# The seam between feed-forward 0 and attention 1: parts of q and k handed over piece by piece, and the first maxima multiplied one block earlier

## The reference

```
x = x + ffn0(layernorm(x))        # gate, up and down projections; every operand is rounded to
                                  # 4-bit floats in blocks of 16 first; hidden width 352
x = x + attention1(layernorm(x))
    q, k, v = x Wq, x Wk, x Wv    # 16 heads of 8 features
    a = q k^T / sqrt(8), causal mask, softmax over keys
    out = (a v) Wout
```

## Time and profile before

| what | value |
|---|---|
| time, median of 3 runs | 934.86 us (933.84 to 935.25) |
| profiled execution: time, span | 932.55 us, 930.8 us |
| PE busy | 842.5 us (91%) |
| DVE busy | 728.3 us (78%) |
| ACT busy | 528.7 us (57%) |
| POOL busy | 465.4 us (50%) |
| mean granted clock of TensorE | 0.98 |

### The profile page before, as it was taken

How to read it: one execution, slowest core, us unless ns; L and a number is a source line. 1 busy time by engine, 2 the same in 40 slices (tenths; PEclk the granted TensorE clock), 3 DMA queues, 4 the chain that set the end, 5 groups by cost and what they waited for, 6 DMA issues and landing times. The chain is left out here.

```text
span 930.8 us, 17280 instructions
## 1 busy us (share of the span) xinstructions
PE 842.5 (91%) x5977; PEld 556.6 (60%) x5977; DVE 728.3 (78%) x1455; ACT 528.7 (57%) x771; POOL 465.4 (50%) x620
## 2 busy tenths in 40 slices
PE   5899999999778886689999999888889999999997
PEld 4677777775566655334444444443558767776875
DVE  6888998879899995888898998987666656565542
ACT  4677788789566675367777777767423223222311
POOL 4133222224568786236666666456464365345444
PEclk9999999999999999779999999999989999999999
DMA  9300000000000006765545446200000000000000
GB/s 284 93 12 12 11 11 11 0 13 0 16 1 12 1 12 130 142 129 117 111 82 126 106 85 127 52 4 14 12 1 24 1 23 23 23 0 23 11 12 12
DMA packets 36067, 43.79 MB, mean 47 GB/s; under 512 B 4878, under 2 KB 28094, under 8 KB 36000
## 3 DMA queue, kind: packets, MB, share of 16 engines
q1 hardware_dynamic: 36000, 42.93, 19.5%
HBM read 21.81 MB, written 15.09 MB: 40 GB/s over the span
## 5 line engine op out<-in xcount | busy, mean ns | idle before, releaser
L1877 ACT ACTIVATE PT<-PS 128x1024 f32<-128x1024 f32 x160 | 161.5, 1022 | 61.6 <-PE PS L1668 61.3
L1939 POOL TENSOR_SCALAR_AFFINE_SELECT PT<-PT 128x256 f32<-128x256 f32 (+1 forms) x224 | 97.3, 451 | 101.9 <-ACT PT L1877 99.9
L2368 POOL TENSOR_TENSOR PRE_sb<-PRE_sb,VA 128x512 f32<-128x512 f32 x64 | 82.3, 1285 | 125.8 <-DVE PRE_sb L2436 125.7
L2335 ACT ACTIVATE sg_d<-PS 128x512 f32<-128x512 f32 x64 | 38.1, 597 | 154.5 <-PE PS L1397 154.5
L2436 DVE TENSOR_TENSOR PRE_sb<-sg_d,PS 128x512 f32<-128x512 f32 x64 | 44.0, 688 | 79.6 <-ACT sg_d L2335 79.1
L465 ACT ACTIVATE E<-PS,m 128x512 f32<-128x512 f32 x128 | 85.7, 688 | 34.7 <-PE PS L351 25.8
L1979 DVE TENSOR_REDUCE negm<-PS 128x2 f32<-128x1024 f32 x64 | 77.8, 1221 | 20.0 <-PE PS L1657 19.6
L1684 PE MATMUL PS<-PT,VA 128*32 128x512 f32 (+3 forms) x1024 | 89.9, 446 | 3.6 <-POOL PT L1939 3.6
L1650 PE MATMUL PS<-kS,qS 52*128 52x384 bf16 (+3 forms) x512 | 64.3, 311 | 14.7 <-ACT PT L1877 6.9
L514 POOL TENSOR_SCALAR Qs<-Qs 128x1024 f32<-128x1024 f32 x32 | 34.5, 1080 | 81.6 <-ACT Qs L446 81.0
L1668 PE MATMUL PS<-qS,kS 55*128 55x384 bf16 (+3 forms) x512 | 63.4, 307 | 7.5 <-DVE negm L1979 3.5
(11 more groups left out here) (331 smaller groups left out, 2249.5 us busy)
## 6 DMA issues: line engine op xcount, KB each, us to landing
qk_rows<-parts SPq DMA_DIRECT2D x32, 192.0 KB, 2.8
qS<-qk_rows SPq DMA_DIRECT2D x32, 192.0 KB, 4.3
kS<-qk_rows SPq DMA_DIRECT2D x32, 192.0 KB, 4.6
xs_sb<-XN_sb SPq DMA_DIRECT2D x20, 256.0 KB, 2.3
qk_rows<-parts SPq DMA_DIRECT2D x32, 128.0 KB, 2.8
X_sb<-in_x_dram SPq DMA_DIRECT2D x8, 256.0 KB, 6.6
qk_rows<-parts SPq DMA_DIRECT2D x32, 64.0 KB, 2.5
out_dram<-X_sb SPq DMA_DIRECT2D x8, 256.0 KB, 2.3
```

Of the source, the lines that this page charges most:

```text
L1877: nc.scalar.activation(PT[:, quad % 2, u, :], PS[:, b:b + 2, :].rearrange("p b n -> p (b n)"), ACT.Exp).then_inc(exp_ready, 1)
L1939: nc.gpsimd.affine_select(out=v, in_=v, pattern=[[0, 4 if u == 4 else 2], [1, P]], compare_op=ALU.is_ge, fill=0.0, base=0, channel_multipl ...
L2368: nc.gpsimd.tensor_tensor(acts[:, s, f, :], acts[:, s, f, :], W[:, slot, s, :], ALU.mult).then_inc(weighted, 1)
```

## The change

Five things are changed, all in the seam.

1. The third parts of sequence 0 (`third_part(pool, 0, m)`) move on POOL from behind `rescale_h(LAST - 1, 1)` to before it.
2. A new function `both_parts_to_rows` takes the place of two calls of `parts_to_rows`, for sequences 0, 1 and 2. It issues the same 12 transfers, but in the order in which parts come to exist: behind the first part of q, the first part of k, the second of q, and so on.
3. The first four units of maxima of sequence 0 move into `last_turn` of feed-forward 0 on PE, behind `down(i, 0)`, behind the projection of k, behind `turn_h(i, 1)` and behind `down(i, 1)`. They alternate between the bank pairs 3, 4 and 1, 2. Their reductions stand at the end of DVE's list of that block.
4. In the opening the remaining 16 units are numbered from 4, and the work between them stands behind other units: v of sequence 0 behind 4, the turn of x behind 5, the projections behind 7 and 9, the turn of the maxima behind 11, v of sequence 1 behind 13 instead of 8. The ring of bank pairs runs the other way round.
5. On ACT `keep_v(0, 0)` stands behind the second parts of sequence 1 instead of before them, and `keep_maxima(0, 0)` before `keep_v(1, 1)` and two constants instead of behind them.

```diff
+    def both_parts_to_rows(self, sp, n, slot):
+
+        for k, part in ((1, self.part1), (2, self.part2), (3, self.part3)):
+            for m in range(2):
+                sp.wait_ge(part, n * 2 + m + 1)
+                t, copies, p = ((0, 3, 0), (3, 2, 1), (5, 1, 2))[k - 1 if m == 0 else 3 - k]
+                for par in range(2):
+                    own = slice(64 * par, 64 * par + 64)
+                    src = self.parts[own, 0, p, :].unsqueeze(1).broadcast_to([64, copies, S]) if m == 0 else self.parts[own, 1, 0:copies, :]
+                    sp.dma_start(self.qk_rows[slot, m, par, 8 * t:8 * (t + copies), :].rearrange("(t e) (a s) -> (e a) t s", t=copies, a=NPAIR),
+                                 src).then_inc(self.parts_out, 16)
...
+            def first_maxima(n):
+                if n >= 2:
+                    pe.wait_ge(pr.max_read, n - 1)
+                maxima_products(nc, g, 0, *OPENING[n], opening_pair(n))
...
                 pe.wait_ge(out_kept, i * 2)
                 down(i, 0)
+                pe.wait_ge(h_made, i * 2 + 2)
+                pe.wait_ge(pr.rows_in[0], 64)
+                first_maxima(0)
                 pe.wait_ge(out_kept, i * 2 + 1)
                 pr.project(pe, 1, 1, g.wk1, pr.k_ready)
+                pe.wait_ge(h_rounded, i * 2 + 2)
+                first_maxima(1)
                 turn_h(i, 1)
+                first_maxima(2)
                 pe.wait_ge(pr.kf_ready, 2)
                 down(i, 1)
+                first_maxima(3)
...
+                if i == LAST - 1:
+                    for m in range(2):
+                        pr.third_part(pool, 0, m)
                 rescale_h(i, 1)
-            for m in range(2):
-                pr.third_part(pool, 0, m)
...
+            for n in range(SOONER):
+                dve.wait_ge(pr.max_ready, n + 1)
+                reduce_maxima(nc, g, *OPENING[n], opening_pair(n))
...
 def ring(n):
 
-    return n % 3
+    return (1 - n) % 3
+OPENING = [(n // 5, n % 5) for n in range(NUNIT)]
+SOONER = 4
+def opening_pair(n):
+
+    return 1 - n % 2 if n < SOONER else ring(n - NUNIT)
...
-            for n, (quad, u) in enumerate(STEPS):
-                if n >= 3:
+            for n in range(SOONER, NUNIT):
+                quad, u = OPENING[n]
+                if n > SOONER:
                     pe.wait_ge(max_read, n - 2)
-                maxima(0, 0, quad, u, ring(n - NUNIT))
-                if n == 0:
+                maxima(0, 0, quad, u, opening_pair(n))
+                if n == 4:
                     project_v(0, 0)
-                elif n == 2:
+                elif n == 5:
                     pe.wait_ge(v_ready, 1)
                     pr.turn_x(pe, 2)
-                elif n == 4:
+                elif n == 7:
                     pr.project(pe, 2, 0, g.wq1, q_ready)
-                elif n == 6:
+                elif n == 9:
                     pe.wait_ge(qf_ready, 3)
                     pr.project(pe, 2, 0, g.wk1, k_ready)
-                elif n == 8:
+                elif n == 11:
                     pe.wait_ge(kf_ready, 3)
-                    project_v(1, 1)
-                elif n == 11:
-                    pe.wait_ge(v_ready, 2)
                     pe.wait_ge(consts, 1)
                     turn_maxima(0, 0)
+                elif n == 13:
+                    pe.wait_ge(m_row, 1)
+                    project_v(1, 1)
...
             nc.scalar.preload_act_table_set("exp_and_others")
-            keep_v(0, 0)
             for m in range(2):
                 pr.second_part(act, 1, m)
+            keep_v(0, 0)
...
             pr.keep(act, 2, 1, k_ready, kf_ready)
+            keep_maxima(0, 0)
             keep_v(1, 1)
...
-            keep_maxima(0, 0)
```

More of the change, by code:

```diff
@@ L1496, in diagonal, with operands, maxima_products, reduce_maxima @@
     return bank.rearrange("p (r n) -> p r n", n=2 * P)[:, :, P:]
+def operands(pr, slot, quad, j, rows):
+    own = slice(64 * (j % 2), 64 * (j % 2) + rows)
+    return pr.qS[own, slot, 2 * quad + j // 2, :], pr.kS[own, slot, 2 * quad + j // 2, :]
+def maxima_products(nc, g, slot, quad, u, pair):
+    pr, PS = g.projection, g.PS
+    for j, col, k in UNIT_MAX[u]:
+        q, key = operands(pr, slot, quad, j, MAX_ROW)
+        W, bank = (k + 1) * P, PS[:, 1 + 2 * pair + j % 2, :]
+        nc.tensor.matmul(bank[:, col:col + W], q[:, k * P:(k + 1) * P], key[:, 0:W], start=(col == 0), stop=False)
+    for half in range(2):
+        for par in range(2):
+            rows = slice(64 * par, 64 * par + 64)
+            steps = pr.halves[rows, 2 + half, 64 * half:64 * half + 64]
+            squares = diagonal(PS[:, 1 + 2 * pair + par, :], u)[:, :, 64 * half:64 * half + 64]
+            n = len(UNIT_MAX[u]) // 2
+            ins = nc.tensor.matmul(squares, pr.halves[rows, half, :], steps.unsqueeze(1).broadcast_to([64, n, 64]), start=False, stop=(half == 1))
+    ins.then_inc(pr.max_ready, 1)
+def reduce_maxima(nc, g, quad, u, pair):
+    negm, PS, b = g.projection.negm, g.PS, 1 + 2 * pair
+    if u < 2:
+        ins = nc.vector.tensor_reduce(negm[:, 3, :, 2 * quad + u], PS[:, b:b + 2, :], AX.X, ALU.max, negate=True)
+    elif u < 4:
+        own = 2 * quad + u - 2
+        nc.vector.tensor_reduce(negm[:, 2, :, own], PS[:, b:b + 2, 0:384], AX.X, ALU.max, negate=True)
+        ins = nc.vector.tensor_reduce(negm[:, 0, :, own], PS[:, b:b + 2, 384:512], AX.X, ALU.max, negate=True)
+    else:
+        ins = nc.vector.tensor_reduce(negm[:, 1, :, 2 * quad:2 * quad + 2], PS[:, b:b + 2, :].rearrange("p b (r n) -> p b r n", r=2),
+                                      AX.X, ALU.max, negate=True)
+    ins.then_inc(g.projection.max_read, 1)
 def in_periods(eng, period):
@@ L1646, in maxima @@
                     pe.wait_ge(rows_in[quad // 2], i * 64 + 64)
-                for j, col, k in UNIT_MAX[u]:
-                    q, key = operands(slot, quad, j, MAX_ROW)
-                    W, bank = (k + 1) * P, PS[:, 1 + 2 * ring_pair + j % 2, :]
-                    nc.tensor.matmul(bank[:, col:col + W], q[:, k * P:(k + 1) * P], key[:, 0:W], start=(col == 0), stop=False)
-                for half in range(2):
-                    for par in range(2):
-                        rows = slice(64 * par, 64 * par + 64)
-                        steps = halves[rows, 2 + half, 64 * half:64 * half + 64]
-                        squares = diagonal(PS[:, 1 + 2 * ring_pair + par, :], u)[:, :, 64 * half:64 * half + 64]
-                        n = len(UNIT_MAX[u]) // 2
-                        ins = nc.tensor.matmul(squares, halves[rows, half, :], steps.unsqueeze(1).broadcast_to([64, n, 64]),
-                                               start=False, stop=(half == 1))
-                ins.then_inc(max_ready, 1)
+                maxima_products(nc, g, slot, quad, u, ring_pair)
             def scores(i, slot, quad, u, ring_pair):
@@ L1736, in period @@
                         if first:
[L1737 removed]
+                            pe.wait_ge(v_ready, 2)
                         elif i <= LAST - 2:
@@ L2129, in period @@
                         mask_first_low(1)
-            for n, (quad, u) in enumerate(STEPS):
-                maxima(0, quad, u, ring(n - NUNIT))
+            for n in range(SOONER, NUNIT):
+                quad, u = OPENING[n]
+                maxima(0, quad, u, opening_pair(n))
                 if u == 4 and quad % 2:
```

35 lines of the change are left out of this document (10 added, 25 removed).

## The result

| | before | changed |
|---|---|---|
| time, median of 20 runs each | 933.81 us | 930.63 us |
| profiled execution: time, span | 932.55, 930.8 | 930.92, 929.2 |

The ratio of the times is 0.9957, with a 95% interval of 0.9940 to 0.9974: 4.0 us faster (2.4 to 5.6); the medians differ by 3.2. Of the 2.1 between forecast and median, 1.05 is the base: the three runs shown before had their median at 934.86, the twenty at 933.81. From the base of twenty the same forecast reads 931.6 and its range begins at 929.9, so the miss is as much the base as the kernel; the other 1.0 is the change, forecast at 2.2 and 3.2 by the medians.

A forecast was written before the change was run, and what follows sets the result against it. DVE was taken to bound the opening of attention 1, the quantisation chain of `hh` the last turn. A lead of 2.3 at unit 8 less 0.1 for v gave -2.2: 934.86 to 932.7 us, range 930.9 to 935.8.

The forecast's parts named there:

- Third parts sooner: Last turn, POOL: third parts before the rescale of `hh(6,1)` delay PE's turn by 2.1 and the tail by 1.8.
- Transfers part by part: SP: parts issued as ready bring the first half's rows in by 360.9, 3 us before unit 0 wants them.
- Four units: Last turn: units 0 and 2 cost 0, unit 1 0.4; unit 3's reduction ends the block 1.3 later.
- the price of the block's end: Start of attention 1: ACT's first instruction comes 1.0 after the block's last instruction ends.
- The clock: TensorE: granted clock assumed high in the last turn and low (half) again in the opening for turn of x and projection.
- the third rival: Clock falls in the last turn, back for the opening's second half: +3.2, lead -0.9, 935.8 us; chance 0.08.
- the first rival: Opening runs at full clock: unit 8 at 380.0, lead 3.5, 931.4 us; chance 0.20.
- The turn of x: Opening, PE: turn of x of sequence 2 waits for `v_ready` instead of the staging transfer, starting at 376.5.
- v of sequence 1 behind unit 13: Opening, PE: projection covered by two reductions; at low clock a gap up to 0.5, taken as 0.1.
- The gift: Last turn, DVE: L180 takes 0.88 instead of 1.18 without the third parts beside it, -0.3.

The follow-up runs named there:

- e3: Changed kernel with no units of maxima in the last turn, all 20 in the opening; 930.38 us, ratio 0.9964 to the kernel before.
- e7: Changed kernel without units in the last turn and with the third parts back behind the rescale of `hh(6,1)`; 926.33 us, ratio 0.9923 to the kernel before.
- e9: e7 with one unit of maxima (unit 0) put back into the last turn, behind the turn of `hh(7,1)`; 923.97 us, ratio 0.9902 to the kernel before.
- e6: Kernel before with only the part transfers of sequences 0, 1 and 2 issued as each part is ready; 927.31 us, ratio 0.9922.
- e1: Changed kernel with the third parts of sequence 0 back behind the rescale of `hh(6,1)`; 931.14 us, ratio 0.9982 to the kernel before.
- e8: Changed kernel with 14 idle transposes before the turn of `hh(6,1)` and 14 before that of `hh(7,0)`; 931.67 us, ratio 0.9973 to the kernel before.
- e10: Changed kernel run once more, unaltered, on one chip with e9; 930.22 us, ratio 0.9948 to the kernel before.
- e2: Changed kernel with `keep_v(0, 0)` on ACT before the second parts of sequence 1; 927.19 us, ratio 0.9929 to the kernel before.
- e5: Changed kernel with `keep_v(0, 0)` on ACT before the exponential table's load and the second parts; 929.23 us, ratio 0.9960 to the kernel before.
- e4: Changed kernel with 14 idle transposes on TensorE in the gap before the turn of `hh(6,1)`; 930.28 us, ratio 0.9949 to the kernel before.

## Why the forecast fell short, point by point

- *Third parts sooner*: right in size and sign. +2.1 at the turn, -0.3 at L180, +1.9 at POOL's rescale of `hh(7,1)` (forecast +1.8); e3 against e7 gives 1.9 in the seam.
- *Transfers part by part*: right that the rows and the staged x stop being waited for. The rows went out where I had them (355.42, which is 354.6 in the times of the trace before; forecast 354.5), and the staging transfer at 359.15, right behind the last of them. What I didn't see is that this edit alone removes both waits even with the late third parts: with the third parts late, the rows are issued at 358.64 (e7), and with the 6.48 from there to the release, which I had from the earlier trace rows, they are in by 365.1, while attention 1 begins at 368.64 (e9 measures it: rows issued at 354.26, TensorE released at 360.95, so 6.69). e6 shows it. Nothing needed the third parts sooner but unit 0 where the change had put it (e1: a wait of 2.88; e9, behind the turn: 0.24).
- *Four units*: unit 1 costs 0.5 (25.92 in e8 against 25.43 in e3; forecast 0.4), unit 0 and unit 2 nothing, unit 3's reduction ends 1.36 behind the keep (forecast 1.3). So these prices were right, the block's end apart. What I didn't ask is what the units are worth against no units: e3, without them, has the shorter seam.
- **The step that failed** is a term of the sum: "ACT's first instruction of attention 1 comes at 368.66, 1.0 after that keep ended: the price of the block's end". The price is 0.35. In the changed kernel attention 1 begins 0.35 behind the last reduction; with no unit 3 (e3, e6, e7) it begins 0.34 behind the keep. Before it was 1.01, because the keep wasn't last: with the transfers issued sooner and nothing else changed (e6) 0.67 of it went. SP's issue at 367.39, 0.55 long, is what I see near the end that e6 moved; that the block waited for it is inferred from this, not tried by itself. In e6 the same issue stands at 362.27. I charged 1.0 behind the new last instruction, 0.65 too much. e8, which has the forecast's clocks, shows it without their errors: attention 1 begins +3.05 there, where I had +3.6, and the lead is 43.50 - 40.53 = 3.0.
- *The clock*: both of the forecast's assumptions were wrong in the profiled execution, and they cancelled by luck. The clock was low in the last turn (+1.2 to 1.4 on the chain, the third rival) and high in the opening (3.42 from the turn of x to unit 8 against 4.65 in e8: -1.2, the first rival). I had treated them as separate cases with chances of their own, and gave their coming together no weight. The third rival's price was wrong too: I laid 5.3 of matmuls on the chain and got 3.2 for the fall, where the runs show 1.2 to 1.4; by its own sum the lead would have been -0.9, and with this fall it was 2.8 (e10: 43.50 - 40.69) and 3.0.
- *The turn of x*: the wait for `v_ready` took the place of the staging transfer's, as forecast: 4.18 behind the block's begin, forecast 4.3. *v of sequence 1 behind unit 13* cost nothing, even at the low clock.
- The sum with 0.35 for 1.0 and nothing for v would have been -3.0, which is the seam's and near the medians' 3.2. In the changed kernel's own profile that agreement leans on the two errors of the clock; in e8 it doesn't. The rest of the ratio's 4.0 (2.4 to 5.6) is within its interval.

The changed kernel's clock fell at 356, behind a wait of 1.91. e2, e3, e5 and e10 waited 1.90 to 1.96 in the same place and didn't fall there; e2, e4 and e10 fell at 361 to 364, behind waits of 1.50 and 0.73, and e3 and e5 had those waits too and didn't fall. So no run here tells which gap does it. The Trainium skill ("TensorE: Matmul & The Clock Gate", HAM oscillation) has it that a wait for a transfer between two groups of matmuls throttles the clock, so that each group starts slow. The waits it tells of are longer than any that stand before a fall in the last turn of these four runs, so they don't bear it out and don't refute it.

The gift, worked out from the row of 326.39, came whole: L180 took 0.88 once the third parts were done. The Trainium skill ("SBUF — State Buffer", Who interferes with whom) has a DVE instruction with two SBUF inputs contend with a POOL instruction that reads SBUF, the later one being blocked. The trace agrees that the two disturb each other, since the 0.3 went with the overlap, but not in size: the overlap was 0.43, and in the changed kernel an L180 at 341.98, wholly beside the first rests (340.81 to 344.05), took 1.05.

## What to carry to other kernels

Take a change of several edits apart before judging it: here issuing the transfers as their data come to exist was worth 5.5 us, moving the work that makes the data sooner cost 1.9 because it stood in front of the engine chain that sets the end, and work moved ahead of a block's end was worth its time only where the engine was waiting and its consumer was idle (e9), not where it stood between two matmul groups of the chain (unit 1) or became the last thing to end (unit 3). Before paying to make something earlier, ask how early it is wanted once its queue is cleared. And a gap between the last visible instruction and the next block isn't a price of the block's end until every queue, SP's too, is known to be done.

## What the runs showed of the hardware

- The next block began 0.34 to 0.35 us behind the last compute instruction of feed-forward 0 in every run where SP's issues were done before; with an SP issue ending at 367.94 (the kernel before) it was 0.72 behind that.
- The granted clock fell at different places in executions with the same instructions: at 356 in the changed kernel and at 361 in its second profile. A fall in the last turn cost 1.2 to 1.4 us on the chain, one in the opening 1.2 (e8), and one in the middle of the opening, where DVE is the limit, nothing (e3: low from 374 to 377, DVE unbroken).
- The times of the changed kernel lie between 925.3 and 934.3 us over 20 runs, seven of them below 926.5 and none from there to 930.0; the seam, read from one profile against a fixed instruction ahead of it, repeated to 0.2.
- Part of that spread is made ahead of the seam, where the computing engines have the same instructions in all these kernels. The first of these rows is from e9 and the second from the changed kernel, the same projection of an earlier turn:

```profile
...
261.80 2.53 PE L982 MATMUL PS<-low_space_sb,xT_sb 128*128 128x352 f32 x8
...
```

```profile
...
264.88 3.67 PE L982 MATMUL PS<-low_space_sb,xT_sb 128*128 128x352 f32 x8
...
```

Both traces have the same matmul at 256.2, behind a wait of 2.7. In the changed kernel the clock then fell to 0.50 from 257 to 267, and the projection came 3.1 later; in e9 it stayed at 1.00. The seam began at 336.12 and 336.27 in the two profiled executions without a fall there (e5 and e9) and between 339.16 and 341.87 in the eleven with one. So a time of one execution can differ by 3 to 6 us for a reason that has nothing to do with the seam, and small gains here are better read from the seam than from few times.
